# x1 of layer 0 moved from VectorE to ScalarE, and one spectrum copy moved ahead of x's high part

## The reference

```
norm  = (sum(adj, -1) + 1e-6) ** -0.5
f_hom = adj @ ((x @ theta) * norm) * norm
f_het = x @ W_h
gate  = sigmoid(x @ W_t + b_t)
out   = elu(gate * f_hom + (1 - gate) * f_het)
x1    = layernorm(x + out)            # (y - mean) / sqrt(var + 1e-5), per node over 256 features
```

## Time and profile before

| | us |
|---|---|
| median of 3 runs | 1990.43 (1988.78 to 1994.69) |
| the profiled execution | 1989.04 |
| its span | 1986.9 |
| `phase_a`, first 486 us: PE busy | 442.08 |
| DVE busy | 411.66 |
| ACT busy | 374.90 |
| POOL busy | 300.82 |

### The profile page before, as it was taken

How to read it: one execution, slowest core, us unless ns; L and a number is a source line. 1 busy time by engine, 2 the same in 40 slices (tenths; PEclk the granted TensorE clock), 3 DMA queues, 4 the chain that set the end, 5 groups by cost and what they waited for, 6 DMA issues and landing times.

```text
span 1986.9 us, 35043 instructions
## 1 busy us (share of the span) xinstructions
PE 1887.1 (95%) x11046; PEld 1653.5 (83%) x11046; DVE 1463.6 (74%) x2972; ACT 1112.3 (56%) x2063; POOL 422.3 (21%) x378
## 2 busy tenths in 40 slices
PE   6999999996999899948999999999999999999997
PEld 6888888885999799947888888888888888888886
DVE  5889888886666788836777777777777777777774
ACT  6878888885666677734444444444444344444442
POOL 4666666664444200000000000000000000000000
PEclk9999999997999999978999999999999999999998
DMA  6777788875333598851212121212121212212200
GB/s 221 251 259 267 273 291 294 289 262 194 101 98 98 188 314 282 279 189 40 100 51 99 49 99 49 92 56 88 60 88 60 82 67 74 75 65 84 78 33 22
DMA packets 184169, 281.13 MB, mean 141 GB/s; under 512 B 14286, under 2 KB 126644, under 8 KB 179860
## 3 DMA queue, kind: packets, MB, share of 16 engines
q1 hardware_dynamic: 184084, 280.10, 41.9%
HBM read 178.60 MB, written 101.45 MB: 141 GB/s over the span
## 4 chain that ended last, share of the span: by engine, by line
PE 53%; issue 1%; DVE 1%; DMA 1%; SPq 0%; ACT 0%; POOLq 0%; POOL 0%; ACTq 0%; DVEq 0%
PE c_ps_g L1539 40%; PE c_ps_m L1517 5%; PE c_ps_m L1548 2%; PE c_ps_y L1574 1%; PE c_ps_m L1550 1%; PE c_ps_y L1632 1%; PE c_ps_m L1632 1%; PE c_ps_m L1549 1%; DMA c_yf<-y_spec 1%; PE c_ps_s L1617 0%; PE c_ps_y L1633 0%; PE c_ps_m L1633 0%; PE c_ps_g L1591 0%; PE c_ps_s L1588 0%; DVE c_wi_l L1482 0%
## 5 line engine op out<-in xcount | busy, mean ns | idle before, releaser
L1308 POOL TENSOR_TENSOR c_rstd<-c_var_eps,c_neg_half 128x4 f32<-128x4 f32 x32 | 32.3, 1008 | 1076.8 <-DVE c_var_eps L1446 1076.8
L1231 ACT ACTIVATE c_yo<-c_ps_y,c_shift,c_rstd 128x256 f32<-128x256 f32 x128 | 61.9, 564 | 169.5 <-DVE c_shift L1454 169.5
L1539 PE MATMUL c_ps_g<-c_ch,c_wi_l 128*128 128x512 f32 x384 | 154.5, 402 | 0.0
L1539 PE MATMUL c_ps_g<-c_nh,c_wi_l 128*128 128x512 f32 x384 | 153.2, 399 | 0.0
L1539 PE MATMUL c_ps_g<-c_xh,c_wh_l 128*128 128x512 f32 x384 | 152.0, 396 | 0.0
L1539 PE MATMUL c_ps_g<-c_xl,c_wh_h 128*128 128x512 f32 x384 | 151.9, 396 | 0.0
L1539 PE MATMUL c_ps_g<-c_ch,c_wi_h 128*128 128x512 f32 x384 | 151.6, 395 | 0.0
L1539 PE MATMUL c_ps_g<-c_xh,c_wh_h 128*128 128x512 f32 x384 | 151.6, 395 | 0.0
L1539 PE MATMUL c_ps_g<-c_cl,c_wi_h 128*128 128x512 f32 x384 | 151.5, 394 | 0.0
L1539 PE MATMUL c_ps_g<-c_nl,c_wi_h 128*128 128x512 f32 x384 | 151.1, 394 | 0.0
L1539 PE MATMUL c_ps_g<-c_nh,c_wi_h 128*128 128x512 f32 x384 | 150.8, 393 | 0.0
(11 more groups left out here) (219 smaller groups left out, 6187.9 us busy)
## 6 DMA issues: line engine op xcount, KB each, us to landing
w_spec<-a_spec SPq DMA_DIRECT2D x32, 1088.0 KB, 8.2
m_w<-w_spec SPq DMA_DIRECT2D x34, 1024.0 KB, 8.3
a_xt<-in_x_t SPq DMA_DIRECT2D x64, 256.0 KB, 3.3
a_xn<-in_x_n SPq DMA_DIRECT2D x64, 256.0 KB, 5.0
x_t<-a_x1t SPq DMA_DIRECT2D x64, 256.0 KB, 4.4
s_x<-x_t SPq DMA_DIRECT2D x64, 256.0 KB, 3.0
y_spec<-x_spec SPq DMA_DIRECT2D x64, 256.0 KB, 5.7
c_x<-x_t SPq DMA_DIRECT2D x32, 512.0 KB, 4.1
```

The lines of the kernel that those rows point to most:

```text
L1231: nc.scalar.activation(yo[:, b], ps_y[:, b], ACT.Identity, bias=shift[:, b:b + 1], scale=rstd[:, b:b + 1]).then_inc(s_yo, 1)
L1308: nc.gpsimd.tensor_tensor(rstd[:, :], var_eps[:, :], neg_half[:, :], ALU.pow).then_inc(s_rstd, 1)
L1539: last = nc.tensor.matmul(out, stationary, moving, start=(count == 0), stop=(count == total - 1))
```

## The change

x1 = (y - mean) * rstd was made by VectorE in two instructions of 256 columns (L548). Now VectorE makes only `nb` = -mean * rstd for both graphs (one instruction of 2 columns, line 554 of the changed kernel), with its own semaphore `s_nb`, and ScalarE makes x1 = rstd * y + nb in two ACTIVATEs with Identity, whose bias is the column `nb` and whose scale is the column of `roots`. They stand between `x1t` and the gate's tanh. Semaphore `s_x1` is now set by ScalarE: VectorE's `y` and `nb`, GpSimd's roots and PE's transposes wait for it as before, and ScalarE waits for `s_nb` and for the transposes that read the same buffer two pairs before. Beside that ScalarE's copy of the fourth spectrum moves from behind `xh` to ahead of it.

```diff
+        nb = sb("nb", [P, 2, 2])
...
@@ scalar: step @@
+                if ahead(7):
+                    spectra_out(t - 7, 3)
                 if live(1):
...
                     nc.scalar.activation(xh[:, v], xt[:, r], ACT.Copy).then_inc(s_xh, 1)
-                if ahead(7):
-                    spectra_out(t - 7, 3)
-                if live(1):
-                    p = i - 1
-                    r = (n - 1) % RING
                     reached(act, s_hom, p - 1)
                     nc.scalar.activation(ah[:, v], at[:, r], ACT.Copy).then_inc(s_ah, 1)
...
                     nc.scalar.activation(x1t[:, v], ps_t[:, :, :], ACT.Copy).then_inc(s_x1t, 1)
+                if live(6):
+                    p = i - 6
+                    reached(act, s_nb, p + 1)
+                    reached(act, s_xp, p - 1)
+                    for b in range(2):
+                        last = nc.scalar.activation(x1[:, u, b], y[:, u, b], ACT.Identity, bias=nb[:, u, b:b + 1], scale=roots[:, u, 2 + b:3 + b])
+                    last.then_inc(s_x1, 1)
@@ vector: step @@
                 if live(6):
                     reached(dve, s_root, p6 + 5)
-                    reached(dve, s_xp, p6 - 1)
-                    for b in range(2):
-                        last = nc.vector.scalar_tensor_tensor(x1[:, u, b], y[:, u, b], mv[:, u, b, 0:1], roots[:, u, 2 + b:3 + b].to_broadcast([P, D]),
-                                                              ALU.subtract, ALU.mult)
-                    last.then_inc(s_x1, 1)
+                    reached(dve, s_x1, p6 - 1)
+                    nc.vector.scalar_tensor_tensor(nb[:, u], mv[:, u, :, 0], -1.0, roots[:, u, 2:4], ALU.mult, ALU.mult).then_inc(s_nb, 1)
```

More of the change, by code:

```diff
@@ L198, in phase_a @@
         s_ve = sem("var_eps_done")
+        s_nb = sem("mean_scaled")
         s_x1 = sem("x1_done")
```

## The result

2000.75 us (median of 7 runs, 1999.74 to 2004.38) against 1990.43: ratio 1.0051, 95% interval 1.0038 to 1.0063, 10.3 us slower. The profiled execution took 2002.16 us (span 2000.4), 13.1 more than that of before. The next phase's first ScalarE instruction starts at 499.33 instead of 487.41, so 11.9 of these 13.1 are `phase_a`'s. The rest of the span, 1501.1 against 1499.5 us, is not touched by the change; single runs of one kernel differ by more than that (1999.74 to 2004.38).

The account below looks back on a forecast made before the run. Bound: the 7.06 us tanh-to-tanh loop through ScalarE and PE, becoming 7.28 through held `nb`. 59 x 0.22 = 13.0 plus the drain's 1.5 gives +14.5 on the profiled 1989.04: 2003.5 us, range 1982 to 2010.

Parts of the forecast that it names:

- the likeliest case: Whole kernel: `nb` held, the pair of x1 at 0.92 to 0.98 us, edges within 2: 2000 to 2008 us.
- the sum: `phase_a`: 59 steps x 0.22 = 13.0 us, 0 for the few steps before, 1.5 for the drain: +14.5 us.
- The hold of `nb`: VectorE's `nb` gets through only when GpSimd's `al` ends, 3.23 us after `xl`'s start, and ends 0.01 later.
- the loop: Tanh to tanh in `phase_a` through copy, `xh`, `xl`, `al`'s end, `nb` and the x1 pair: 7.28 us, against 7.06.
- my reading of `yo`: Price of ScalarE's x1 pair, taken from `phase_c`'s four ACTIVATEs of the same form: 0.94 us.
- ScalarE's wait for `nb`: ScalarE ahead of the first x1: ready at 5.96 us after the tanh, `nb` at 6.34, a wait of 0.38.
- PE's waits: PE waits 0.3 to 0.4 us at the gate's bias for `gd` (held `sums_eps`), about 0.25 at the first spectrum.
- The drain's 1.5: End of `phase_a`: last x1 go from 0.88 to about 1.3 us on the chain, three times: 1.5 us.
- The copy ahead of xh: ScalarE's fourth copy earlier: by itself removes PE's whole 0.41 us wait at the first spectrum, 6.65 us per step.
- the first and third rivals: First: `nb` not held, 6.96 per step, 1982 to 1985, chance 0.14. Third: held, pair 0.66, 7.00, 1987, chance 0.10.
- The turning point: Sign of the change: below an x1 pair of 0.72 us the forecast's loop is shorter than 7.06.
- The rule on the port: VectorE with two SBUF inputs against GpSimd reading SBUF: whoever comes first keeps the shared port, the other fully blocks.

Follow-up runs that it names:

- nb_free: Changed kernel, but `nb` made by two VectorE instructions of one column with one tensor input each; 1990.42 us, ratio 1.0003 to the kernel before.
- swap_only: Kernel before with only the fourth spectrum's copy moved ahead of `xh`, x1 staying on VectorE; 1989.84 us, ratio 0.9999.
- nb_ve_columns: Changed kernel with `nb` and the variance's `sums_eps` each as two tensor_scalar of one column; 1984.86 us, ratio 0.9967 to the kernel before.
- x1_plain: Changed kernel with x1's two ACTIVATEs as plain copies of y, without column operands; 1988.17 us, ratio 0.9991 to the kernel before.
- swap_ve_x1_free: Kernel before with the fourth copy ahead of `xh`, the variance's `sums_eps` as one two-column tensor_scalar, x1 as two tensor_scalar on VectorE; ratio 0.9996.

## Why the prediction was right, and where it was not

The forecast was slower by 13 us from the median, 2003.5; it is 10.3, 2000.75, within the 2000 to 2008 of the likeliest case and the whole range of 1982 to 2010. By the profiles, `phase_a` lost 11.9 us where 14.5 were forecast, so the sum was a little too long. That the medians differ by 10.3 and not by 11.9 is within the interval of the ratio (7.6 to 12.5 us).

**The hold of `nb`** is shown: by its duration and its end beside `al`, and by nb_free, which takes the hold away, leaves ScalarE's work as it is and gets all the loss back. That the loop came out at 7.25 for 7.28 is in part luck, two errors against each other: x1 starts 0.04 after `nb`, not 0.12, and the pair is 1.00, not 0.94. The Trainium skill (ScalarE: Activation LUTs, What ACT_TABLE_LOAD costs) led to an estimate of 0.98 for the pair, and that was nearer to the measured 1.00 than my reading of `yo`. ScalarE's wait for `nb` was forecast at 0.38 and is 0.27 by starts (0.80 from `x1t` to x1, less 0.53).

**PE's waits** came as forecast: at the bias behind `gd` (0.05 after its end), and 0.28 still at the first spectrum (308.68 + 0.12 to 309.08), where about 0.25 was forecast.

**The sum**: the last 59 intervals of the tanh add 10.5 us (0.22 each was forecast, 13.0), the four before them 1.2 where I had put 0. The held `sums_eps` comes in there already: the third interval is 7.05 for 6.60, 7.04 in swap_only too, and 6.57 in nb_ve_columns, where it is not held. Another 0.6 lies ahead of the first tanh (22.8 for 22.2), before any `nb`; the profiled kernels scatter there from 21.4 to 22.8. The drain's 1.5 (three times 1.3 less 0.88 is 1.3, in fact) did not come: at the last tanh the kernel is 12.2 us behind, at the start of the next phase 11.9. Why the drain costs nothing was not looked into.

**The copy ahead of xh** is the step that failed: "by itself this takes away the whole 0.41: 6.65 us per step". swap_only shows 7.03. Two things were missing in that sentence: the held `sums_eps` makes `gd` late (I used it for PE's wait, not for the swap alone), and a copy moved ahead of `xh` makes `xh` wait for PE's fourth spectrum. In the changed kernel the tanh is late enough to hide the second. For the same reason the first and third rivals' 6.96 and 7.00 were too low: nb_free and x1_plain end at 7.03. The turning point was too low for another: by the measured loop (7.25 with a pair of 1.00) it is a pair of 0.81, not 0.72.

**The rule on the port**: The Trainium skill (SBUF — State Buffer, Who interferes with whom) says that of two instructions which both need the shared port, the one that starts first keeps it for its whole length and the other blocks. The trace agrees, in both directions (`nb` 0.63 for 0.15 behind `al`, `al` 0.94 for 0.74 behind x1). The same section of the Trainium skill also lists tensor_scalar among the instructions that contend when their operands allow the two-port mode; I passed that by. swap_ve_x1_free shows it, with its `sums_eps` of 0.65 us.

## What to carry to other kernels

A tiny instruction can set the step (the hold of `nb` cost 7.25 against 7.03): look for places where a short instruction takes much longer than its twin, and see what ends at the same time. Before work is moved to the engine with the most free time, add up every loop from one step to the next, through waits for a shared port too; an edit that shortens the longest loop gains only the distance to the next one, which was 0.03 us here. Two edits that are each worth nothing alone may be worth 0.8% together.

## What was new about the hardware

VectorE and GpSimd do not meet at semaphores alone: 59 of the 64 `nb` of the changed kernel took over 0.6 us where the other five took 0.15 or 0.16, though nothing in the program lets `nb` wait for `al`. A tensor_scalar of two columns is held by a GpSimd instruction that reads SBUF too (0.65 us beside `xl`), one of one column is not (0.20 for two). A two-input instruction issued directly behind a held one gets ahead of the next GpSimd instruction in the queue (0.15 us, 0.01 ahead of `res`), one issued 0.13 after GpSimd has started waits until it is over (0.63).
